# A selective scan whose Delta, B and C come from one product, with B and C spread by DMA

## The reference

```
xi    = silu(conv1d(in_w[:96] @ x))            # (L = 1024, 96 channels)
dbl   = xi @ xp_w.T                            # 6 ranks for Delta, 16 B, 16 C
delta = softplus(dt_w @ dbl[:6] + dt_b)        # (L, 96)
dA    = exp(delta * A)                         # (L, 96, 16 states)
dBu   = delta * B * xi
h     = dA * h + dBu                           # along L
y     = sum over states of h * C
out   = out_w @ ((y + D * xi) * silu(z))
```

## Time and profile before

| | |
|---|---|
| median of three runs | 4404.16 us (4399.27 to 4412.59) |
| the profiled execution, its own time | 4406.85 us |
| its span, first to last instruction | 4405.1 us |
| mean granted TensorE clock | 0.938 of full speed |
| busy: PE, DVE, ACT, POOL | 3987.6, 3400.8, 2901.3, 2380.0 us |
| DMA, mean over the span | 131 GB/s |

### The profile page before, as it was taken

The page is one execution under the profiler, slowest core; times in us unless marked ns, Lnnn a source line. Parts: engine busy times, 40 slices in busy tenths (PEclk is TensorE's granted clock), DMA queues, the critical chain, the costliest instruction groups (busy, mean ns, idle before and its releaser), DMA issues.

```text
span 4405.1 us, 42054 instructions
## 1 busy us (share of the span) xinstructions
PE 3987.6 (91%) x14264; PEld 1462.3 (33%) x14264; DVE 3400.8 (77%) x2997; ACT 2901.3 (66%) x3476; POOL 2380.0 (54%) x1108
## 2 busy tenths in 40 slices
PE   6889997999879998799987999889998899978997
PEld 2332234222342223422244222432234322342223
DVE  1469977799668996599965998669977699667996
ACT  1577747677577765767666775767757777476664
POOL 0137752577426874177732787228762477425773
PEclk9989999899899999899998999989989899898888
DMA  1147651667417763277624775257742576506671
GB/s 43 44 122 191 172 136 45 168 171 186 98 53 181 184 173 84 80 179 178 171 60 109 181 179 136 76 129 179 182 122 67 136 190 171 124 16 168 157 177 42
DMA packets 166830, 579.12 MB, mean 131 GB/s; under 512 B 22572, under 2 KB 23320, under 8 KB 163064
## 3 DMA queue, kind: packets, MB, share of 16 engines
q1 hardware_dynamic: 152280, 538.67, 48.8%
q10 hardware_dynamic: 14336, 37.76, 2.8%
HBM read 467.12 MB, written 71.48 MB: 122 GB/s over the span
## 4 chain that ended last, share of the span: by engine, by line
PE 65%; DVE 16%; ACT 10%; issue 5%; DMA 2%; POOL 0%; SPq 0%; DVEq 0%; POOLq 0%; ACTq 0%
PE ps L775 15%; PE ps L796 9%; PE ps L842 9%; DVE arena L1456 6%; PE ps L691 6%; PE ps L678 5%; DVE ps L1451 4%; PE ps L788 3%; PE ps L549 3%; PE ps L609 3%; PE ps L685 3%; PE ps L805 3%; ACT arena L940 2%; ACT arena L922 2%; PE ps L600 2%
## 5 line engine op out<-in xcount | busy, mean ns | idle before, releaser
L1538 POOL TENSOR_TENSOR arena<-arena 128x1024 f32<-128x1024 f32 x768 | 1803.0, 2357 | 890.5 <-DVE arena L1456 890.5
L1456 DVE TENSOR_TENSOR_SCAN arena<-arena,ps 128x1024 f32<-128x1024 f32 x768 | 1756.4, 2287 | 34.6 <-ACT arena L1145 8.3
L1451 DVE TENSOR_TENSOR ps<-ps,arena 128x1024 f32<-128x1024 f32 x768 | 933.0, 1215 | 220.8 <-PE ps L777 219.5
L1145 ACT ACTIVATE arena<-arena,a_all 128x1024 f32<-128x1024 f32 x768 | 865.8, 1141 | 318.5 <-DVE arena L1456 252.0
L775 PE MATMUL ps<-arena,spread 32*128 32x512 f32 x1536 | 909.7, 674 | 83.2 <-DVE arena L1456 83.2
L777 PE MATMUL ps<-arena,spread 32*128 32x512 f32 x1536 | 908.7, 674 | 0.0
L796 PE MATMUL ps<-arena,gather 128*32 128x512 f32 x3072 | 541.8, 652 | 4.5 <-POOL arena L1538 4.5
L842 PE MATMUL ps<-x 96*96 96x512 f32 x1008 | 505.6, 620 | 0.0
L775 PEld LDWEIGHTS ps<-arena,spread 32*128 32x128 f32 x1536 | 234.7, 190 | 727.4 <-issue 449.0
L1501 POOL TENSOR_TENSOR x<-x,arena 96x512 f32<-96x512 f32 x64 | 113.9, 1779 | 369.3 <-DVE arena L1321 369.3
L897 ACT ACT_TABLE_LOAD x226 | 290.0, 1283 | 24.9 <-DMA wo<-in_wo 20.9
(11 more groups left out here) (152 smaller groups left out, 5164.8 us busy)
## 6 DMA issues: line engine op xcount, KB each, us to landing
arena<-dl SPq DMA_DIRECT2D x768, 512.0 KB, 5.3
dl<-arena ACTq DMA_DIRECT2D x64, 384.0 KB, 5.8
x<-pn SPq DMA_DIRECT2D x56, 247.5 KB, 6.8
arena<-in_x SPq DMA_DIRECT2D x9, 1536.0 KB, 14.0
arena<-xq SPq DMA_DIRECT2D x64, 192.0 KB, 5.8
arena<-arena ACTq DMA_DIRECT2D x64, 192.0 KB, 5.0
out<-x SPq DMA_DIRECT2D x64, 192.0 KB, 2.1
arena<-xq SPq DMA_DIRECT2D x64, 191.8 KB, 5.1
```

Of the source, the lines that this page charges most:

```text
L1145: act.activation(da[:, m % DAS, :], dbc[:, m % DBC, :], ACT.Exp, scale=a_all[:, v // 2, m:m + 1]).then_inc(da_ready, 1)
L1451: dve.tensor_tensor(driven, driven, bmat[:, v % 2, :], ALU.mult).then_inc(bu_ready, 1)
L1456: dve.tensor_tensor_scan(hs[:, m % HSS, :], da[:, m % DAS, :], driven, 0.0, ALU.mult, ALU.add).then_inc(h_ready, 1)
L1538: pool.tensor_tensor(product, product, cmat[:, v % 2, :], ALU.mult).then_inc(pr_ready, 1)
```

## The change

One product per half gives Delta's input and B and C: the weights w_dbc have 96 + 32 columns, and the result fills 128 rows of banks 6 and 7. Softplus reads rows 0 to 95, and one copy (keep_bc) brings rows 96 to 127 into bc, which lies in the free rows of Delta's tile. SP spreads the sixteen rows of B and of C from there, each row to eight partitions, into bmat and cmat. These two transfers stand in slots 7 and 8 of SP, the window loads of the convolution go from slot 8 to slot 10, and Delta's write to DRAM from slot 6 to slot 4. DVE and POOL wait for the transfers where they waited for ACT's copies; PE's waits on those copies become waits on keep_bc.

```
-PE_DT, PE_B, PE_C, PE_OUT = 3, (5, 6), (7, 8), (9, 10)
-ACT_SILU, ACT_DL, ACT_U = 1, 6, 8
-ACT_DT, ACT_B, ACT_C, ACT_OUT = 4, (6, 7), (8, 9), (10, 11)
+PE_DBC, PE_OUT = 3, (9, 10)
+ACT_SILU, ACT_ROWS, ACT_U = 1, 4, 8
+ACT_DBC, ACT_OUT = 4, (10, 11)
+SP_B, SP_C = 7, 8
-SP_STORE, SP_LOAD = 3, 8
+SP_STORE, SP_LOAD = 3, 10
...
-        delta = cut(DI, L)
+        delta_bc = cut(128, L)
+        delta, bc = delta_bc[0:DI], delta_bc[DI:128]
...
+                def spread_state(v, k, dst, landed, freed):
+                    V = p * UNITS + v
+                    sync.wait_ge(bc_ready, V + 1)
+                    if v >= 2:
+                        settled(sync)
+                        sync.wait_ge(freed, (V - 1) * G)
+                    sync.dma_start(dst[:, v % 2, :],
+                                   bc[k * NS:(k + 1) * NS, :].rearrange("n (o t) -> n o t", o=1)
+                                   .broadcast_to([NS, DG, L])).then_inc(landed[v % 2], 16)
...
                 def first():
-                    for m in range(DBC):
-                        spread_delta(0, m)
+                    spread_delta(0, 0)
+                    spread_b(0)
+                    spread_delta(0, 1)
+                    spread_c(0)
+                    spread_delta(0, 2)
...
-                def of_xi(rows, bank, weights, i, c):
-                    return pe.matmul(ps[0:rows, bank, :], weights, xi[:, i, c * 512:(c + 1) * 512],
+                def of_xi(q, i, c):
+                    return pe.matmul(ps[:, 6 + c, :], w_dbc[:, q, :], xi[:, i, c * 512:(c + 1) * 512],
                                      start=True, stop=True)
...
-                    if slot in PE_B:
-                        c = PE_B.index(slot)
...
-                        of_xi(128, 6, xp_rep[:, q, 0, :], i, c).then_inc(b_ps, 1)
-                    if slot in PE_C:
-                        c = PE_C.index(slot)
...
-                        of_xi(128, 6, xp_rep[:, q, 1, :], i, c).then_inc(c_ps, 1)
+                            of_xi(q, i, c).then_inc(dt_ready, 1)
...
                             if v + 1 < UNITS:
-                                pe.wait_ge(delta_ready, 2 * (p * UNITS + v + 2))
+                                pe.wait_ge(bc_ready, p * UNITS + v + 2)
...
+                def keep_bc(v):
+                    V = p * UNITS + v
+                    act.wait_ge(dt_ready, 2 * V + 2)
+                    if v:
+                        act.wait_ge(b_in[(v - 1) % 2], (p * QUADS + (v - 1) // 2 + 1) * 16)
+                        act.wait_ge(c_in[(v - 1) % 2], (p * QUADS + (v - 1) // 2 + 1) * 16)
+                    act.activation(bc, two(6)[DI:128], ACT.Copy).then_inc(bc_ready, 1)
...
-                    if slot == ACT_DT:
+                    if slot == ACT_DBC:
                         softplus(v)
                         exp_table()
...
+                        keep_bc(v)
...
                     if m == 0:
-                        dve.wait_ge(b_ready, 2 * V + 2)
+                        dve.wait_ge(b_in[v % 2], (p * QUADS + v // 2 + 1) * 16)
...
                     if m == 0:
-                        pool.wait_ge(c_ready, 2 * V + 2)
+                        pool.wait_ge(c_in[v % 2], (p * QUADS + v // 2 + 1) * 16)
```

More of the change, by code:

```diff
@@ L442, in prep @@
                         shifted(v + 1)
+                    if v and slot == SP_B:
+                        spread_b(v)
+                    if v and slot == SP_C:
+                        spread_c(v)
                 def first():
-                    for m in range(DBC):
-                        spread_delta(0, m)
+                    spread_delta(0, 0)
[3 more added lines that the diff above has]
+                    spread_delta(0, 2)
                 def step(v, m):
@@ L701, in prep_first @@
                         pe.wait_ge(xi_ready, 2 * V + c + 1)
-                        of_xi(DI, 6 + c, wdt_all[:, 0, :], 0, c).then_inc(dt_ready, 1)
-                    for c in range(2):
-                        of_xi(128, 4 + c, xp_rep[:, 0, 0, :], 0, c).then_inc(b_ps, 1)
+                        of_xi(0, 0, c).then_inc(dt_ready, 1)
                     for c in range(2):
@@ L714, in first @@
                     broadcast_u(0, 0)
-                    for c in range(2):
-                        of_xi(128, c, xp_rep[:, 0, 1, :], 0, c).then_inc(c_ps, 1)
                 def prep(slot, v):
@@ L1063, in softplus @@
                                        bias=small_all[:, v // 2, KC + 1:KC + 2]).then_inc(delta_ready, 1)
-                def keep_b(v, c, bank):
+                def keep_bc(v):
                     V = p * UNITS + v
-                    act.wait_ge(b_ps, 2 * V + c + 1)
-                    if v >= 2 and c == 0:
-                        act.wait_ge(bu_ready, (V - 1) * G)
-                    act.activation(part(bmat[:, v % 2, :], c), ps[:, bank, :], ACT.Copy).then_inc(b_ready, 1)
-                def keep_c(v, c, bank):
-                    V = p * UNITS + v
-                    act.wait_ge(c_ps, 2 * V + c + 1)
-                    if v >= 2 and c == 0:
-                        act.wait_ge(pr_ready, (V - 1) * G)
-                    act.activation(part(cmat[:, v % 2, :], c), ps[:, bank, :], ACT.Copy).then_inc(c_ready, 1)
+                    act.wait_ge(dt_ready, 2 * V + 2)
[3 more added lines that the diff above has]
+                    act.activation(bc, two(6)[DI:128], ACT.Copy).then_inc(bc_ready, 1)
                 def delta_to_rows(v):
@@ L1101, in early @@
                         exp_table()
-                    if slot == ACT_DT:
+                    if slot == ACT_DBC:
                         softplus(v)
                         exp_table()
-                    if slot in ACT_B:
-                        keep_b(v, ACT_B.index(slot), 6)
-                    if slot in ACT_C:
-                        keep_c(v, ACT_C.index(slot), 6)
+                        keep_bc(v)
                 def prep_first():
@@ L1115, in prep_first @@
                     delta_to_rows(0)
-                    for c in range(2):
-                        keep_b(0, c, 4 + c)
+                    keep_bc(0)
                     move_u(0)
@@ L1133, in prep @@
                         exp_table()
-                    if slot == ACT_DL:
+                    if slot == ACT_ROWS:
                         delta_to_rows(v)
@@ L1148, in first @@
                 def first():
-                    decay(0, 0)
-                    for c in range(2):
-                        keep_c(0, c, c)
-                    for m in range(1, DAS - 1):
+                    for m in range(DAS - 1):
                         decay(0, m)
```

41 lines of the change are left out of this document (15 added, 26 removed).

## The result

The changed kernel takes **4545.13 us** (median of four runs, 4542.90 to 4570.08), the kernel before 4406.75 in the same comparison: a ratio of **1.0326, 95% interval 1.0292 to 1.0360**. It is 3.3% slower; the forecast was 4384, 0.5% faster.

What follows compares the result with a forecast made beforehand. PE was taken as full in steady units, with DVE close behind at a floor of 41.36 us. Relief of -44 and pair starts of +24 gave -20, hence 4384 us against the median 4404.16; 8-in-10 range 4322 to 4448.

Steps and rivals of the forecast that it cites:

- DVE waits 2p - 8.2 us per unit, [...] nothing below 4.1: Steady units: DVE's wait for the next unit's first Delta block behind the spreads; 0.8 us at p = 4.5.
- The taps' wait: Convolution taps on PE wait for the copy of B and C, not Softplus alone: 1.2 us once per unit.
- The third rival: Copy for B and C delays step 6's Exp by 1.0 us, taps by 1.2: 4402, no change; chance 0.13.
- The price p: Time of one 512 KB spread on SP's queue: 4.5 us taken, between bounds of 2.24 and 9.1.
- The slower rival: DMA queue becomes the bound: at p = 5.5 DVE waits 2.8 us per unit, 4448 us; chance 0.21.
- The head: Start of each pair: first scan starts p later behind B's spread, net +3.0 us per pair, +24 over eight.
- the gain of 1.5 us later in unit 0: In each pair's first unit, DVE wins back 1.5 of 1.66 us lost to PE's load, without B and C.
- PE's relief, -44: Steady units without the B and C products take 43.13 us each, 2.08 less per two units, over seven pairs.
- The sum of relief and head, -20: Whole kernel: -44 in steady units and +24 at pair starts, taken from the profiled 4406.85 us, giving 4387.

Runs made afterwards that it cites:

- the fourth block: Changed kernel with four buffers for Delta blocks instead of three, so SP may issue each block one step earlier: 4420.79 us, ratio 1.0030 to the kernel before.
- the moved Gelu: Changed kernel with ACT's Gelu of slot 10 written ahead of the Exp of the next unit's step 0: 4588.61 us, ratio 1.0435 to the kernel before.
- the fastest version: Changed kernel with B and C by way of DRAM, four Delta blocks, copy of B and C ahead of the table load: 4380.48 us, ratio 0.9940.
- run 7: Not a label: "in one run", then 7 of 28 waits. That run: changed kernel, four Delta blocks, four unread products per unit, 4580.15 us.

## Why the prediction was wrong

- **The step that failed** is "DVE waits 2p - 8.2 us per unit, [...] nothing below 4.1". Its formula for the landing was right: 4.8 + 3 x 2.24 + 2 x 3.45 = 18.4 us after the issue, and 18.42 were measured. DVE was indeed not held by that block. But the step priced only one reader's due time. The Exp that waits for the block stands at the head of ACT's list, and PE's product needs the Gelu behind it; that second due time is earlier than DVE's: in the unit shown the Exp was due at 879.08 for DVE, but at some 873.7 (its end at 876.43, less PE's wait of 2.73) for PE. That the late blocks cost the time is shown by the fourth block (125 us), the spreads left out (126 us) and the DRAM source (83 us); that they do it through ACT's list, by the moved Gelu, with which PE waits for the next thing that ACT does. With B earlier PE waits in part for a transfer of ACT's own that lands late, so the load of the queue reaches PE in a second way too.
- **What a wait of PE costs.** The taps' wait was forecast at 1.2 us per unit; it was 0.6 on average in the change (24.3 us in 42 units) and 1.44 in the bad unit with four blocks. It was priced at its own length, but where the clock falls to half behind it, for 10 us and more, the unit takes up to 7 us more. Moving one copy by 1.28 us was worth 147 us with PE full. The third rival had the wait, with a price several times too small.
- **The price p** was 3.45 us, below the 4.5 taken and inside the bounds of 2.24 and 9.1. The sentence from the Trainium skill, "SBUF — State Buffer", section "Door 1: The DMA port swizzle", gave an estimated 5.0, from its 104 GB/s for sixteen partitions; the measured 152 GB/s decides.
- **The slower rival** had the right sign and the wrong mechanism: it needed p over 5.3 and DVE waiting. At 3.45 it predicted a gain.
- **The head**: +24 forecast, +40 found. The first scan is late by p, as stated, 3.54 us; the gain of 1.5 us later in unit 0 isn't there, and some 1.5 us more are lost instead.
- **PE's relief, -44.** The row it was read from was right on average: forecast were 43.13 us a unit, and units 1 to 5 take 43.1 with the later spreads left out and 43.3 in the fastest version (43.8 before), with a clock that falls where PE gets room. They do so unevenly: units 1 and 2 gain nothing, units 3 and 4 take 84 to 86 together. In the change itself a unit takes 47.1. The sum of relief and head, -20, is near what the fastest version shows (-26), but in part by luck, since its spreads come from DRAM and its heads cost some 10 us rather than 24; the change as it stands never gets there.

Open: how the loss splits between these two ways; why the clock fell for 10 us and more behind 7 of 28 equal waits of PE, for some 3 us behind 13 and not at all behind 8; why units 1 and 2 stay at a clock of 0.93 in the fastest version; and the change with three blocks and the earlier copy wasn't tried, so that what the taps' wait costs in the change itself isn't shown.

## What to carry to other kernels

When a transfer gets later, don't ask only whether its reader's result is still in time: go down the reader's own list and ask who waits for each instruction behind it. Price a wait of an engine that was full not at its length, but at its length and what the granted clock does afterwards, read from the nearest stretch with such a wait. Give a queue that gets more transfers one more buffer, and place a copy that frees a bank ahead of a table load, before judging the idea itself.

## What the runs showed of the hardware

- Of two spreads out of SBUF that SP issues 1.3 us apart, the second holds SP for 4.34 us at the start of a pair and 3.50 in the unit shown, a median of 4.0 over the change, and ACT for 2.85 where ACT issues it. Issued 6.5 us apart, in the run with B in slot 6 and C in slot 9, it takes 0.56 us, and from DRAM 0.55.
- 512 KB out of sixteen SBUF partitions to 128 take 3.45 us, out of DRAM 2.5 for B and C, if the Delta blocks between them keep the 2.24 that they take back to back.
- Of 28 PE waits of 1.4 us in one run 7 were followed by 10 to 17 us at half the clock, 13 by some 3 us and 8 by none; in the change 27 of 28 waits of 1.6 to 4.6 us were followed by 7 to 14 us. Products that nobody reads cost 63 and 159 us on top of four blocks where PE's wait for the copy stood, and 12 where it didn't.
